# The last module's second gate, moved from the attention into the state-space loop in four units of 256 columns

## What is computed

```python
x = x + attention(gate0(x, f));   x = x + ternary_ffn(gate1(x, f))
x = x + state_space(gate2(x, f)); x = x + mixture_of_experts(gate3(x, f))
# gate(r, f, w, u, time_emb), with k = v = f:
ek = exp(min(f, 30)); ekv = ek * f
nf, nb = decaying sums of ekv over the tokens, forward and backward; df, db = the same of ek
num = nf + nb - ekv + min(exp(u + f), e^30) * f
den = df + db - ek + min(exp(u + f), e^30)
gate = sigmoid(x) * num / max(den, 1e-8) * (0.8 + 0.2 * tf)
```

## Time and profile before

| | |
|---|---|
| Runs | 737.68, 734.25 and 737.98 us, median 737.68 |
| Profiled execution | 735.4 us, its span 733.6 us |
| Mean granted TensorE clock | 0.887 |
| Busy over the span | PE 572.9, PEld 434.9, DVE 403.4, ACT 375.1, POOL 153.5 us |
| Attention | about 45 to 249 us |
| State-space loop | about 376 to 502 us |
| Expert blocks | about 535 to 715 us |

### The profile page before, as it was taken

One profiled execution on the slowest core, in us unless ns is written; L12 is line 12 of the kernel. 1 busy time (PEld: TensorE's weight loads), 2 busy tenths in 40 slices (PEclk: granted clock), 3 DMA queues, 4 the chain that ended last, 5 costly groups with the idle time before them and its releaser, 6 DMA issues.

```text
span 733.6 us, 14233 instructions
## 1 busy us (share of the span) xinstructions
PE 572.9 (78%) x5820; PEld 434.9 (59%) x5822; DVE 403.4 (55%) x586; ACT 375.1 (51%) x799; POOL 153.5 (21%) x121
## 2 busy tenths in 40 slices
PE   0176967578767766669999999987489999999990
PEld 0043645445545642445555665656389999999990
DVE  5889899679897377955745554524611111211113
ACT  6986878449876507654666555553212222222212
POOL 1000000000001028621058544300012223222210
PEclk9995588785888998898999999998579999999996
DMA  9400000000001000000000000000498888988815
GB/s 355 150 1 1 1 1 1 1 1 0 1 2 30 1 0 1 0 1 1 2 2 4 2 2 3 2 3 30 152 361 311 330 331 304 333 332 313 339 51 179
DMA packets 18480, 72.18 MB, mean 98 GB/s; under 512 B 4528, under 2 KB 9776, under 8 KB 14704
## 3 DMA queue, kind: packets, MB, share of 16 engines
q1 hardware_dynamic: 15120, 64.19, 23.9%
q0 software_dynamic: 2208, 6.03, 2.1%
q10 hardware_dynamic: 1088, 1.05, 0.4%
HBM read 66.16 MB, written 5.11 MB: 97 GB/s over the span
## 4 chain that ended last, share of the span: by engine, by line
PE 59%; DVE 22%; ACT 11%; issue 4%; DMA 2%; POOL 1%; SPq 0%; ACTq 0%; DVEq 0%; POOLq 0%
PE PS L1348 48%; DVE nmx L991 3%; DVE arena L904 3%; DVE arena L901 3%; ACT arena L591 2%; PE PS L1401 2%; PE PS L1386 1%; PE PS L1599 1%; PE PS L1417 1%; ACT arena L578 1%; DVE A L923 1%; PE PS L1464 1%; DMA arena<-ypair 1%; ACT arena L751 1%; DVE arena L1095 1%
## 5 line engine op out<-in xcount | busy, mean ns | idle before, releaser
L1348 PE MATMUL PS<-arena 128*128 128x128 f32 (+5 forms) x1682 | 194.1, 290 | 17.4 <-DVE arena L1095 10.1
L1348 PEld LDWEIGHTS PS<-arena 128*128 128x128 f32 (+3 forms) x1684 | 162.3, 170 | 43.0 <-issue 25.7
L1322 DVE TENSOR_TENSOR R<-arena,PS 128x128 f32<-128x128 f32 x23 | 6.6, 288 | 135.1 <-ACT arena L832 135.1
L591 ACT ACTIVATE arena<-PS,nmx 128x128 f32<-128x128 f32 (+1 forms) x128 | 52.2, 425 | 44.4 <-DVE nmx L991 44.4
L1401 PE MATMUL PS<-ident,arena 128*128 128x128 f32 x192 | 38.6, 357 | 32.6 <-ACT arena L578 30.5
L1348 PE MATMUL PS<-arena,R 128*128 128x256 f32 x276 | 63.5, 380 | 0.6 <-ACT arena L838 0.6
L1348 PEld LDWEIGHTS PS<-arena,R 128*128 128x128 f32 x276 | 50.6, 190 | 6.9 <-issue 0.9
L1401 PEld LDWEIGHTS PS<-ident,arena 128*128 128x128 f32 x192 | 30.2, 186 | 39.9 <-ACT arena L591 25.9
L462 POOL DMA_INDIRECT ypair<-arena,oid x23 | 22.8, 991 | 135.9 <-ACT arena L838 135.9
L372 POOL TENSOR_SCALAR arena<-ident,gcol 128x128 f32<-128x128 f32 x4 | 2.4, 603 | 233.2 <-DMA gcol<-in_gcol 233.2
L432 POOL TENSOR_TENSOR arena<-arena 128x1024 f32<-128x1024 f32 x16 | 37.8, 2369 | 40.5 <-DVE arena L1177 32.5
(11 more groups left out here) (271 smaller groups left out, 1130.1 us busy)
## 6 DMA issues: line engine op xcount, KB each, us to landing
arena<-in_moe SPq DMA_DIRECT2D x23, 1408.0 KB, 6.7
arena<-in_moe SPq DMA_DIRECT2D x23, 768.0 KB
inproj<-in_inproj SPq DMA_DIRECT2D x1, 1344.0 KB, 10.6
arena<-in_fT SPq DMA_DIRECT2D x1, 1024.0 KB, 5.1
xT<-in_xT SPq DMA_DIRECT2D x1, 1024.0 KB, 5.5
R<-in_w1T SPq DMA_DIRECT2D x1, 1024.0 KB, 7.5
R<-in_w2T SPq DMA_DIRECT2D x1, 1024.0 KB, 9.5
R<-in_w3T SPq DMA_DIRECT2D x1, 1024.0 KB, 11.6
```

The lines of the kernel that those rows point to most:

```text
L591: sc.activation(pr[u % 2][:, j, 0:n], PS[:, 2 * (u % 2) + j // 2, (j % 2) * 256:(j % 2) * 256 + n], ACT.Exp, bias=nmx[:, u % 2, j:j + 1], ...
L1348: last = mm(dst, l, r, start=(n == 0), stop=(n == len(pairs) - 1))
```

## The change

Only seven gate halves (`GATES`) are computed in the attention. The eighth, i = 7, is cut into four units, t = 0 to 3, one for each pair of feature group and batch. A unit has 256 columns. Unit t is computed in the iterations 2t and 2t + 1 of the state-space loop, and its last three operations come in iteration 2t + 2 (for unit 3 behind the loop). f lies no longer in SBUF by then, so SP loads the unit's 256 columns again (128 KB) into one of two buffers. The decay is not written out as a matrix: the scans read one column, broadcast. The gb and gcol loads wait for one gate half less and so start earlier.

```diff
+        uf = [ekvq[:, 512 + T * i:512 + T * (i + 1)] for i in range(2)]
+        uek, ufc, uxe, uxv = [dmats[0][:, T * i:T * (i + 1)] for i in range(4)]
+        ug, unf, udf, udb = [dmats[1][:, T * i:T * (i + 1)] for i in range(4)]
...
-            sp.wait_ge(S["dve_R"], 8)
-            sp.wait_ge(S["act_euk"], 16)
+            sp.wait_ge(S["dve_R"], 7)
+            sp.wait_ge(S["act_euk"], 14)
...
+            sp.wait_ge(S["dve_num"], 7)
+            for t in range(4):
+                ct, n, cols = unit(t)
+                if t:
+                    sp.wait_ge(S["act_uin"], 3 * t)
+                load(uf[t % 2], a["fT"][:, 1, cols], "unit")
...
-                    if u + 4 * c < 7 * FRAME:
+                    if u + 4 * c < (GATES - 1) * FRAME:
                         gate_part(u + 4 * c)
...
+            def unit_inputs(t):
...
+                done(sc.activation(uek, uek, ACT.Exp))
+                sc.activation(uxe, uek, ACT.Copy, scale=dq[:, 3, ct, n:n + 1]).then_inc(S["act_uin"], 1)
+                sc.activation(ufc, uf[t % 2], ACT.Copy, scale=cb[:, n:n + 1]).then_inc(S["act_uin"], 1)
+                sc.activation(ug, uf[t % 2], ACT.Exp, bias=wu[:, 3, 1, ct:ct + 1]).then_inc(S["act_uin"], 1)
+
+            def unit_guess(t):
+                act.wait_ge(S["dve_uden"], t + 1)
+                done(sc.activation(udb, udf, ACT.Relu, bias=tiny[:, 0:1]))
+                done(sc.activation(udb, udb, ACT.Ln, bias=tiny[:, 1:2]))
+                sc.activation(udb, udb, ACT.Exp, scale=-1.0).then_inc(S["act_uguess"], 1)
...
                     inverse_root(i - 1)
+                if i % 2 == 0:
+                    unit_inputs(i // 2)
+                else:
+                    unit_guess(i // 2)
                 if i == NT - 2:
                     sigmoid_x(3, 0)
...
+            def unit_scan(t, x, y):
+                ct, n, cols = unit(t)
+                d = dec[:, 3, ct, n:n + 1].broadcast_to([P, T])
+                done(v.tensor_tensor_scan(y, d, x, 0.0, ALU.mult, ALU.add))
+                done(v.tensor_tensor(y[:, T - 1:T], y[:, T - 1:T], rdq[:, 3, ct, n:n + 1], ALU.mult))
+                done(v.tensor_tensor_scan(y[:, 0:T - 1][:, ::-1], d[:, 1:T], y[:, 0:T - 1][:, ::-1], y[:, T - 1:T], ALU.mult, ALU.add))
+
+            def unit_den(t):
+                dve.wait_ge(S["act_uin"], 3 * (t + 1))
+                unit_scan(t, uxe, udf)
+                done(v.scalar_tensor_tensor(udf, ug, E30, udf, ALU.min, ALU.add), "dve_uden")
+
+            def unit_num(t):
+                done(v.tensor_tensor(uxv, uxe, ufc, ALU.mult))
+                unit_scan(t, uxv, unf)
+                done(v.scalar_tensor_tensor(ug, ug, E30, ufc, ALU.min, ALU.mult))
+                done(v.tensor_tensor(unf, unf, ug, ALU.add), "dve_unum")
+
+            def unit_out(t):
+                ct, n, cols = unit(t)
+                dve.wait_ge(S["act_uguess"], t + 1)
+                done(v.scalar_tensor_tensor(udf, udf, 1e-8, udb, ALU.max, ALU.mult))
+                done(v.scalar_tensor_tensor(udf, udf, 2.0, udb, ALU.subtract, ALU.mult))
+                done(v.scalar_tensor_tensor(R[:, 3, 1, cols], unf, -1.0, udf, ALU.mult, ALU.mult))
...
             for i in range(NT):
...
                 if i + 1 < NT:
                     front(i + 1)
+                if i % 2:
+                    unit_den(i // 2)
+                    unit_num(i // 2)
+                    if i < NT - 1:
+                        unit_min(i // 2 + 1)
+                elif i:
+                    unit_out(i // 2 - 1)
             gate(3, 0)
             gated(NT - 1)
             add_out(NT - 2)
+            unit_out(3)
```

More of the change, by code:

```diff
@@ L128, in build, with unit @@
         wter = arena[:, 27 * K:30 * K].bitcast(BF).rearrange("p (w n) -> p w n", w=3)
+        uf = [ekvq[:, 512 + T * i:512 + T * (i + 1)] for i in range(2)]
+        uek, ufc, uxe, uxv = [dmats[0][:, T * i:T * (i + 1)] for i in range(4)]
+        ug, unf, udf, udb = [dmats[1][:, T * i:T * (i + 1)] for i in range(4)]
+        def unit(t):
+            ct, b = divmod(t, 2)
+            return ct, 2 + b, slice(ct * HALF + b * T, ct * HALF + (b + 1) * T)
         def by_half(o):
@@ L261, in bank @@
             return PS[:, i, 0:n]
-        ld = {k: sem("ld_" + k) for k in ("x", "f", "const", "small", "ffn", "attn", "ssd", "gb", "route")}
+        ld = {k: sem("ld_" + k) for k in ("x", "f", "const", "small", "ffn", "attn", "ssd", "gb", "route", "unit")}
         ld_ring = [sem(f"ld_ring{i}") for i in range(RING)]
@@ L279, in build @@
             act_hgt act_rs dve_dec act_decay pool_pad dve_rinv pe_r act_rT dve_num act_ekq act_ekvq act_sq act_yw
-            dve_hqt dve_iden dve_msq dve_peak pe_rows pe_ss pool_diag pool_osc pool_root""".split()
+            dve_hqt dve_iden dve_msq dve_peak pe_rows pe_ss pool_diag pool_osc pool_root act_uguess act_uin dve_uden
+            dve_umin dve_unum""".split()
         S = {n: sem(n) for n in NAMES}
@@ L382, in out_scales @@
                 t, four = slice(4 * c, 4 * c + 4), [P, 4, 2]
-                pool.wait_ge(S["dve_den"], 8 + c + 1)
+                pool.wait_ge(S["dve_den"], GATES + c + 1)
                 done(pool.tensor_tensor(oscale[:, t, :], den[:, t, :], rms1[:, t].unsqueeze(2).broadcast_to(four), ALU.mult))
@@ L596, in gate_part @@
                 i, k = 1 + n // FRAME, n % FRAME
-                if k == 0 and i < 7:
+                if k == 0 and i < GATES - 1:
                     scaled_inputs(i + 1, 0)
-                if k == 4 and i < 7:
+                if k == 4 and i < GATES - 1:
                     scaled_inputs(i + 1, 1)
@@ L602, in gate_part @@
                     reciprocal_guess(i)
-                if k == 2 and i < 7:
+                if k == 2 and i < GATES - 1:
                     decay(i + 1)
-                if k == 3 and i < 7:
+                if k == 3 and i < GATES - 1:
                     bonus(i + 1)
@@ L770, in inverse_root @@
                 sc.activation(rsb[i % 2], rsb[i % 2], ACT.Exp, scale=-0.5).then_inc(S["act_rs"], 1)
+            def unit_inputs(t):
+                ct, n, cols = unit(t)
+                act.wait_ge(S["dve_umin"], t + 1)
+                if t:
+                    act.wait_ge(S["dve_unum"], t)
+                done(sc.activation(uek, uek, ACT.Exp))
[7 more added lines that the diff above has]
+                sc.activation(udb, udb, ACT.Exp, scale=-1.0).then_inc(S["act_uguess"], 1)
             for q in range(4):
@@ L1218, in add_out, with unit_min @@
                 done(v.tensor_tensor(sl, sl, t2, ALU.add), "dve_x")
+            def unit_min(t):
+                dve.wait_ge(ld["unit"], 16 * (t + 1))
+                if t:
+                    dve.wait_ge(S["act_uin"], 3 * t)
+                done(v.tensor_scalar(uek, uf[t % 2], 30.0, None, ALU.min), "dve_umin")
+            def unit_scan(t, x, y):
[14 more added lines that the diff above has]
+            def unit_out(t):
+                ct, n, cols = unit(t)
+                dve.wait_ge(S["act_uguess"], t + 1)
+                done(v.scalar_tensor_tensor(udf, udf, 1e-8, udb, ALU.max, ALU.mult))
+                done(v.scalar_tensor_tensor(udf, udf, 2.0, udb, ALU.subtract, ALU.mult))
+                done(v.scalar_tensor_tensor(R[:, 3, 1, cols], unf, -1.0, udf, ALU.mult, ALU.mult))
+            unit_min(0)
             dve.wait_ge(S["act_xc"], 6)
@@ L1851 @@
 FRAME = 5
+GATES = 7
 PEAK_BANK = (0, 2, 5, 0)
```

## The result

The changed kernel took 754.27 us (median of 4 runs, 752.31 to 755.83) against 736.99 (4 runs, 734.25 to 737.98): ratio 1.0239, 95% interval 1.0200 to 1.0278, slower by some 17.6 us. The forecast was slower, 747, with 754 as the end of its range, so the result lies just outside. The sign and the mechanism were right; the size was 7 us short.

A forecast was written before the change was run, and what follows sets the result against it. VectorE was taken to lead in the attention, TensorE in the loop. Attention -9.2, stalls +14.0, ScalarE +1.7 and clock +4.5 gave +11.0 us on 735.4: 746.4 to 748.7, stated as 747, range 730 to 754.

The forecast's parts named there:

- What bounds what: VectorE leads in the attention's second half, TensorE in the state-space loop, where VectorE idles half the time.
- The attention, -9.2: Attention ends 9.2 us earlier without gate 7: 1.6 in its first stretch, 7.6 of TensorE's idle time in the second.
- The third rival: Units blocked and the attention gives only 4 us, as waits for ScalarE's copies replace VectorE: +16, 752 to 754; chance 0.08.
- A unit's length, 5.6 us, by itself 0.4 of stall: Loop iterations 1, 3 and 5: a unit takes VectorE 5.6 us, almost fits its idle time; stalls 0.4 if unblocked.
- Blocked by POOL, stalls of 5.2, 6.2 and 2.6: Loop iterations 1, 3, 5: VectorE operations with two SBUF inputs wait for POOL's instructions, stalling TensorE 14.0 us in sum.
- ScalarE, +1.7: Loop iteration 6: unit 3's four inputs stand ahead of the sigmoid and delay the state's copy by 1.7 us.
- Clock, 3 x 1.5 = 4.5: Loop: TensorE returns at half speed after each of three new stalls, costing 4.5 us in all, bounds 0 and 6.
- The rival of no blocking: Loop: POOL doesn't hold unit operations; stalls 0.4, no clock loss, 1.7 on ScalarE: -7.1, 728.3 or some 730; chance 0.20.
- the partly blocked one: Loop: units blocked only in part, stalls of 7 and clock loss of 1: +0.5, no change; chance 0.12.

The follow-up runs named there:

- e_attn: Changed kernel without any unit, its loads or ScalarE's part, so gate half 7 is computed nowhere; against the kernel before: 728.45 us, ratio 0.987.
- e_units: Changed kernel with all eight gate halves kept in the attention and the four units also run in the loop; against the kernel before: 760.09 us, ratio 1.0325.
- The first experiment: Changed kernel's attention side alone, gate half 7 computed nowhere; against the kernel before: ratio 0.987, 9.6 us less.
- e_conv: Changed kernel with unit 0 among the convolutions and the other units one piece per iteration, none in the attention; against the kernel before: 730.78 us, ratio 0.9927.
- e_fill5: Kernel before plus four single-SBUF-input VectorE reductions (4.98 us) in each of iterations 1, 3 and 5; against the kernel before: 736.76 us, ratio 1.0001.
- e_steps_late: Changed kernel with POOL's steps of tiles 4 and 6 held until behind add_out of tiles 0 and 2; against the kernel before: 742.98 us, ratio 1.0084.
- e_fill11: Kernel before plus VectorE reductions of 10.9, 10.9 and 7.5 us in iterations 1, 3 and 5; against the kernel before: 758.14 us, ratio 1.0288.
- e_fill8: Kernel before plus VectorE reductions of 8.4, 7.5 and 7.5 us in iterations 1, 3 and 5; against the kernel before: 748.31 us, ratio 1.0141.
- e_inputs_late: Changed kernel with POOL's steps delayed and ScalarE's inputs of unit 3 moved from iteration 6 to 7; against the kernel before: 745.81 us, ratio 1.0123.

## Why the prediction was short

**What bounds what:** right. The attention follows VectorE and the loop TensorE; e_attn left out VectorE's work in the one and gained, e_units added work in the other and lost only where TensorE came to wait.

**The attention, -9.2:** too much for the changed kernel. The landmarks show 5.7, and e_units against the changed kernel 6.3. The first experiment alone (9.6) would have called the term right; two ways of taking the difference, and e_conv's gain of 5.4, say it was about 6. This is the smaller of the two steps that failed: the hand count of what TensorE keeps as idle time. I left 1.7 us of the 9.3; the window of after has 29.50 - 24.61 = 4.9 left, so this stretch gave 4.7 for 7.6; the one ahead of it gave 1.1 for 1.6. TensorE's timeline has the five waits of before as 1.23, 3.69, 0.42 and 2.01 for ScalarE's copies and 1.94 for an addition to xT; after they are 1.23, 0.21, none and 1.51, and again 1.94. So only the one of 3.69 went nearly whole. The third rival had this in it (4 us, waits for ScalarE's copies) and was nearer. That its 752 to 754 us also come close to the time is in part luck, since it took the prediction's waits and clock as they are.

**A unit's length, 5.6 us, by itself 0.4 of stall:** right. The scans took 0.69 and 0.75 for an estimate of 0.70, a whole unit 5.5, and e_fill5 with 4.98 cost 0.

**Blocked by POOL, stalls of 5.2, 6.2 and 2.6:** the mechanism was right, scans included. Iteration 3 ran in the order that the prediction gave as its alternative, both POOL instructions in a row. The waits were 4.14, 5.56 and 2.22, so 11.9 for 14.0. The Trainium skill (SBUF — State Buffer, "SBUF: two separate sides") has the lock for an operation with two SBUF inputs and for a whole instruction; the traces agree, with a product of one column that took 3.42 us in place of 0.16, and with single-input reductions that kept their 1.22 beside the same POOL work. e_steps_late took POOL's steps away and got 11.4 us back.

**ScalarE, +1.7:** the wait grew by 1.65, as said; that it is a saving to undo it was not shown.

**Clock, 3 x 1.5 = 4.5:** this is the larger of the two steps that failed. The rows showed what follows waits of 2.97 and 3.69 us, and I used their price for waits of 4 to 6. Measured: 4.3 and 4.6 us behind the two longer waits, nothing behind the third, 8.9 in all, with TensorE at the lower level for nearly all of the 10 us each time. e_fill11 shows the same stretches at 0.57 and 0.53 with a different cause of the wait, so they come with the waits and not with the units. A price per wait is wrong in kind as well, as equal waits of 2.2 us cost from nothing to 3.3 in the runs here. My bounds for this term, 0 to 6, were drawn too tight for what the rows had shown.

In sum: predicted +11.0; +3.5 from the attention, -2.1 from the waits, +4.4 from the clock, +0.9 of small terms in the loop and +0.8 between attention and loop give +18.5, where the timed ratio says +17.6.

The rival of no blocking fell (its sum of stalls had to be under 7.5, it was 11.9), the partly blocked one too (7 of stalls and 1 of clock, where it was 11.9 and 8.9).

## To carry to other kernels

Idle time of an engine is a list of gaps with neighbours. Before work is put in one, lay the other engines' timeline over it: here VectorE's gap was exactly POOL's slot, and each of the five unit operations with two SBUF inputs that began while a POOL instruction ran ended only behind it, down to one column. Cut the work into pieces shorter than the slack of each gap, and place them where the partner is quiet. And price a new stall of TensorE at more than its own length: here waits of 4.1 and 5.6 us cost 8.4 and 10.2, and waits of 2.2 cost between 2.2 and 5.6.

## What I had not expected

- The clock behind a wait: after 4.14 and 5.56 us of waiting TensorE worked 9.9 and 10.2 us at 0.54 and 0.52, where after 2.22 us it was at 1.00 at once. But equal waits don't cost the same. In the table each stretch runs from the token transposes to the first product of `within`, and is 5.6 us at full clock. All five waits over 4 us were followed by 9.7 to 10.2; waits of about 2 us by anything from 5.6 to 8.9, and one of 1.45 by 8.9. What else decides stays open.

| run | the three waits, us | stretch behind each, us |
|---|---|---|
| after | 4.14, 5.56, 2.22 | 9.8, 10.2, 5.6 |
| e_units | 2.20, 5.57, 2.23 | 7.2, 9.7, 5.6 |
| e_fill11 | 4.73, 5.61, 2.15 | 9.7, 10.1, 5.6 |
| e_fill8 | 1.98, 2.17, 2.16 | 7.2, 7.2, 8.9 |
| e_steps_late | 1.17, 2.23, 2.23 | 5.6, 5.6, 8.9 |
| e_inputs_late | 1.45, 2.23, 2.23 | 8.9, 8.7, 8.9 |

- The same program's early stages differ by profile: the scan of my first landmark began at 183.33 us in the kernel before, at 185.71 in e_fill5 and at 186.69 in e_fill11, which are the same program up to there. A difference of 2 to 3 us between two single profiles is nothing until it is taken from a landmark behind that.
- The held scan ends 0.54 or 0.55 us behind POOL's instruction (399.96 and 399.41; 444.44 and 443.90), the held one-column product within 0.02.
